# A four-layer conditional network on one core: early blocks in a written-out order, a reordered tail, and 23 products of a constant on TensorE

## The reference, cut to what matters

```python
# x: 16 samples x 128 tokens x 128 features; per sample: two expert numbers, a subject, two angles
h = gelu(x @ Wi[e0] + bi[e0]) @ Wo[e0] + bo[e0] + x         # layer 0, one of 8 experts per sample
x = layernorm(h) * gamma[e0] + beta[e0]
h = layernorm(x) * ln_g + ln_b                              # layer 1
h = (h - mean_over_tokens) / std_over_tokens * gamma(subject) + beta(subject)
gates, idx = top_k(softmax(h @ router_w), 2)                # each token picks 2 of 8 experts
y = sum over the 2 of gate * (relu(h @ w1[e] + b1[e]) @ w2[e] + b2[e])
x = x + y
x = rotate pairs of features by theta and phi               # layer 2
r = gelu(x @ down_W.T + down_b)                             # layer 3, one of 16 experts per sample
x = layernorm((r @ expert_W[e3].T + expert_b[e3] + emb[e3]) @ up_W.T + up_b + x) * gamma3 + beta3
```

## Time and profile before

| | before |
|---|---|
| median of 3 runs (lowest, highest), us | 231.68 (230.59, 233.28) |
| the profiled execution's own time, us | 230.44 |
| its span from the first to the last instruction, us | 228.6 |
| busy: PE, DVE, ACT, POOL, us | 178.3, 116.6, 107.2, 109.0 |
| mean granted TensorE clock, share of full | 0.842 |
| in the chain that ended last: PE, DVE, POOL, issue, DMA | 35%, 21%, 19%, 11%, 9% |

### The profile page before, as it was taken

One profiled execution on the slowest core, in us unless ns is written; L12 is line 12 of the kernel. 1 busy time (PEld: TensorE's weight loads), 2 busy tenths in 40 slices (PEclk: granted clock), 3 DMA queues, 4 the chain that ended last, 5 costly groups with the idle time before them and its releaser, 6 DMA issues.

```text
span 228.6 us, 5312 instructions
## 1 busy us (share of the span) xinstructions
PE 178.3 (78%) x1287; PEld 161.6 (71%) x1287; DVE 116.6 (51%) x575; ACT 107.2 (47%) x338; POOL 109.0 (48%) x126
## 2 busy tenths in 40 slices
PE   6999997999959599284799888887799994077920
PEld 6999986898859599173798777876688873045710
DVE  6316798888943868940023343311236777353460
ACT  3564874665235566301566556564356651123310
POOL 5126335102870670127777777777776333101560
PEclk9999999997667859857589999999999999555555
DMA  6999999994643113047456565535951011330001
GB/s 205 294 322 337 329 317 301 250 292 123 220 130 100 26 34 106 1 104 231 137 154 186 156 173 146 147 97 173 319 167 57 26 46 47 106 134 1 26 25 44
DMA packets 35048, 34.82 MB, mean 152 GB/s; under 512 B 3793, under 2 KB 26475, under 8 KB 35019
## 3 DMA queue, kind: packets, MB, share of 16 engines
q1 hardware_dynamic: 27995, 26.56, 40.3%
q0 software_dynamic: 2496, 5.12, 7.5%
q10 hardware_dynamic: 4528, 2.81, 4.0%
HBM read 29.81 MB, written 4.65 MB: 151 GB/s over the span
## 4 chain that ended last, share of the span: by engine, by line
PE 35%; DVE 21%; POOL 19%; issue 11%; DMA 9%; DVEq 2%; ACT 1%; ACTq 0%; POOLq 0%; SPq 0%
PE bank L808 31%; POOL got L536 7%; POOL token_rows L542 7%; DMA got<-h_rows,src_i 6%; DVE st L1196 3%; PE bank L975 1%; POOL rstd L522 1%; DVE hot_in L1374 1%; POOL rs L556 1%; DVEq L1598 1%; DMA token_rows<-y_blk,dst_i 1%; DMA w_place<-token_rows 1%; DVE y_blk L1475 1%; DVE top_i L1272 1%; PE bank L1004 1%
## 5 line engine op out<-in xcount | busy, mean ns | idle before, releaser
L726 ACT ACTIVATE hid<-bank,small 128x128 f32<-128x128 f32 x156 | 44.4, 368 | 28.0 <-PE bank L808 27.2
L808 PE MATMUL bank<-w,hid 128*128 x312 | 46.5, 297 | 5.3 <-DVE y_blk L1475 4.8
L542 POOL DMA_INDIRECT token_rows<-y_blk,dst_i x39 | 38.8, 995 | 23.0 <-DVE y_blk L1475 13.4
L536 POOL DMA_INDIRECT got<-h_rows,src_i x39 | 38.2, 981 | 22.2 <-issue 10.1
L808 PE MATMUL bank<-gotT,w_now 128*128 128x128 f32 x312 | 46.8, 299 | 0.0
L808 PEld LDWEIGHTS bank<-w,hid 128*128 128x128 f32 x312 | 42.1, 209 | 6.3 <-issue 6.0
L808 PEld LDWEIGHTS bank<-gotT,w_now 128*128 128x128 f32 x312 | 42.9, 213 | 0.0
L1475 DVE TENSOR_TENSOR y_blk<-bank,b_tab 128x128 f32<-128x128 f32 x39 | 11.4, 291 | 58.5 <-PE bank L808 57.0
L975 PE MATMUL bank<-ident,got 128*128 128x128 f32 x39 | 13.0, 334 | 18.0 <-DMA got<-h_rows,src_i 13.2
L716 ACT ACTIVATE gotT<-bank 128x128 f32<-128x128 f32 x39 | 11.0, 282 | 27.2 <-PE bank L975 26.9
L667 ACT ACTIVATE act<-bank,small 128x128 f32<-128x128 f32 x64 | 18.0, 374 | 11.9 <-PE bank L808 11.5
(11 more groups left out here) (232 smaller groups left out, 267.8 us busy)
## 6 DMA issues: line engine op xcount, KB each, us to landing
w_now<-in_exp_w SPq DMA_DIRECT2D x39, 256.0 KB, 3.3
...
```

Source lines behind the costliest of these rows:

```text
L536: g_.indirect_dma_start(got[:, n % RING, :], None, h_dram[0:(HB if n < EARLY else NB) * P], bass.IndirectOffsetOnAxis(ap=src_i[:, n:n + 1] ...
L542: g_.indirect_dma_start(y_dram, bass.IndirectOffsetOnAxis(ap=dst_i[:, n:n + 1], axis=0), y_blk[:, n % YRING, :], None).then_inc(st_y[n % Y ...
L726: last = a_.activation(hid[:, n % HRING, c, :], up_bank(n)[:, c * P:(c + 1) * P], ACT.Relu, bias=cols[:, bass.ds(e * FC + (R_B1 + c), 1)])
L808: return t_.matmul(out_, lhsT, rhs, start=start, stop=stop)
```

## The change

1. Early blocks. What PE, ACT, DVE and POOL do for blocks 0 to 8 and for routing groups 2 and 3 is now written out call by call. DVE no longer adds b2 for these blocks: ACT copies the product (`evac_y`), and POOL adds b2 in `scatter(n)` just before it issues the DMA, with the expert's number loaded into a register first. ACT takes over the normalization of groups 2 and 3 (`norm1`; DVE gives the shift, `minus_mean`). `hot_slots` makes two comparisons of 8 x 128 elements in place of 16 of 128. `experts3(2)` and `experts3(3)`, which prepare layer 3, move behind the early blocks, and the 8 products of `keep_warm` ahead of them are gone. In layer 0 `rows_back` and `store_rows` of groups 0 and 1 come earlier.
2. Tail. BEGIN3 goes from 30 to 34, so units 0 to 3 start four blocks later, and unit 3 ends after the last block. The root of units 1 to 3 and their gain and shift move from DVE to POOL, those of unit 6 from POOL to DVE (`own_norm`). PE loads the experts' numbers of layer 3 ahead of time (`l3_which`). SP stores units 1 to 3 after the last loads.
3. `fill(n)` issues `keep_warm(n)` at six places of the tail: 3 + 12 + 2 + 2 + 2 + 2 = 23 products.

```diff
@@ -50,10 +50,11 @@
-    RING, YRING, TRING, WRING, HRING = 16, 12, 4, 6, 3
+    RING, YRING, TRING, WRING, HRING = 16, 10, 4, 6, 3
...
+    FIRST_OUT = 3
...
@@ -61,7 +62,7 @@
-    BEGIN3 = 30
+    BEGIN3 = 34
...
@@ -468,16 +471,15 @@
-                if n == SETTLED + WRING + 2:
+                if n == SETTLED + WRING + 4:
...
                     for u in range(HU):
                         load_y(u)
-            for u in range(HU):
-                store_out(u)
+            store_out(0)
             scattered(NBLK)
             for u in range(HU, NU):
                 load_y(u)
-            for u in range(HU, NU):
+            for u in range(1, NU):
                 store_out(u)
...
@@ -538,7 +540,14 @@
             def scatter(n):
-                pool.wait_ge(v_y, n + 1)
+                if n < EARLY:
+                    pool.wait_ge(a_y, n + 1)
+                    e = pool.value_load(exp_i[0:1, n:n + 1], min_val=0, max_val=E1 - 1)
+                    ch.do(g_.tensor_tensor(y_blk[:, n, :], y_blk[:, n, :],
+                                           b2_tab[:, bass.ds(e, 1), :].rearrange("p o d -> p (o d)"), ALU.add))
+                    ch.settle()
+                else:
+                    pool.wait_ge(v_y, n - EARLY + 1)
                 g_.indirect_dma_start(y_dram, bass.IndirectOffsetOnAxis(ap=dst_i[:, n:n + 1], axis=0),
                                       y_blk[:, n % YRING, :], None).then_inc(st_y[n % YRING], 16)
...
@@ -578,18 +588,21 @@
-                if n == 2:
+                if n == 3:
                     power(1, 2)
                 if n == 4:
                     power(1, 3)
+                if n == 5:
+                    power(2, 2)
                 if n == 6:
-                    power(2, 2)
-                if n == 7:
                     power(2, 3)
             hot_tiles(1)
-            for n in range(HELD):
+            pool.wait_ge(l_w2, 16 * (E1 + 1))
+            for n in range(FIRST_OUT):
                 scatter(n)
             hot_tiles(2)
+            for n in range(FIRST_OUT, HELD):
+                scatter(n)
             pool.wait_ge(v_idx, 2)
             pool.wait_ge(st_h[2], 16)
             pool.wait_ge(st_h[3], 16)
@@ -599,13 +612,18 @@
                 scatter(n)
                 if n + LEAD < NBLK:
                     gather(n + LEAD)
+            power3(1)
+            power3(2)
+            gain_shift3(1)
+            gain_shift3(2)
+            power3(3)
+            gain_shift3(3)
             power3(HU)
             power3(HU + 1)
             gain_shift3(HU)
             power3(HU + 2)
             gain_shift3(HU + 1)
             power3(HU + 3)
-            gain_shift3(HU + 2)
...
@@ -685,8 +703,8 @@
-                if b == 14:
-                    store_rows(0)
+                if b >= 13 and b < 13 + HG:
+                    store_rows(b - 13)
...
@@ -742,39 +759,61 @@
...
+            def evac_y(n):
+                act.wait_ge(p_y, n + 1)
+                a_.activation(y_blk[:, n, :], y_bank(n), ACT.Copy).then_inc(a_y, 1)
+
             act.wait_ge(v_exp, 1)
-            transposed(0)
-            transposed(1)
-            e = block_expert(0)
-            for k in range(NBLK):
-                if k == EARLY:
-                    transposed(k)
-                    transposed(k + 1)
+            for k in range(EARLY):
+                transposed(k)
+                if k == 2:
+                    norm1(2)
+                if k == 3:
+                    norm1(3)
+                if k == 5:
+                    film_h(2)
+                    film_h(3)
+                hidden(k, block_expert(k))
+                if k >= BEHIND:
+                    evac_y(k - BEHIND)
+                if k == 6:
+                    store_rows(2)
+                if k == 7:
+                    store_rows(3)
+                    hot_rows(1)
+            evac_y(EARLY - 2)
+            evac_y(EARLY - 1)
+            hot_rows(2)
+            evac_m3(2)
+            evac_m3(3)
+            transposed(EARLY)
+            transposed(EARLY + 1)
+            act.wait_ge(v_exp, 2)
+            e = block_expert(EARLY)
+            for k in range(EARLY, NBLK):
...
-                if k == 3:
-                    film_h(2)
-                if k == 4:
-                    film_h(3)
-                    hot_rows(1)
-                if k == 5:
-                    store_rows(2)
-                if k == 6:
-                    store_rows(3)
...
@@ -785,10 +824,15 @@
-                if 2 <= u and odd == 0:
-                    norm3(u - 2)
-            norm3(HU - 1)
+                if k == NBLK - 1:
+                    norm3(0)
+            gelu3(2)
+            evac_uT(3)
+            gelu3(3)
+            norm3(1)
+            norm3(2)
             evac_uT(HU)
+            norm3(3)
             evac_uT(HU + 1)
...
@@ -930,11 +976,11 @@
+                if b == 13:
+                    rows_back(0)
                 if b == 14:
+                    rows_back(1)
                     rank(0)
-                    rows_back(0)
-                if b == 15:
-                    rows_back(1)
...
@@ -962,10 +1010,7 @@
             experts3(0)
             experts3(1)
             inverse(0)
-            experts3(2)
-            experts3(3)
             pe.wait_ge(v_bias, 1)
-            keep_warm(8, bank[6], ident[:])
             pe.wait_ge(l_w2, 16 * (E1 + 1))
...
@@ -1021,9 +1068,15 @@
+            place3 = {}
+
+            def l3_which(u):
+                b, _ = UNITS[u]
+                place3[u] = [pe.value_load(m_idx[0:1, b + k:b + k + 1], min_val=0, max_val=MT - 1) for k in unit(u)]
+
             def l3_up(u):
                 b, n = UNITS[u]
-                which = [pe.value_load(m_idx[0:1, b + k:b + k + 1], min_val=0, max_val=MT - 1) for k in unit(u)]
+                which = place3.pop(u)
...
@@ -1031,52 +1084,72 @@
...
             def down_of(n):
                 e = pe.value_load(exp_i[0:1, n:n + 1], min_val=0, max_val=E1 - 1)
                 blk_down(n, e)
 
-            for k in range(NBLK + BEHIND):
-                if k == EARLY:
-                    down_of(k - 2)
-                    inverse(2)
-                    down_of(k - 1)
-                    pe.wait_ge(v_exp, 2)
-                    rows_T(k)
-                    rows_T(k + 1)
+            pe.wait_ge(v_exp, 1)
+            pe.wait_ge(a_gelu, NB)
+            pe.wait_ge(a_m3, 2)
+            rows_T(0)
...
+            rows_T(3)
+            z_transposes(2)
+            blk_up(3)
+            down_of(1)
+            rows_T(4)
+            z_transposes(3)
+            blk_up(4)
+            down_of(2)
+            rows_T(5)
+            blk_up(5)
+            down_of(3)
+            rows_T(6)
+            route(2)
+            blk_up(6)
+            route(3)
+            down_of(4)
+            rows_T(7)
+            rank(1)
+            rows_back(2)
+            blk_up(7)
+            down_of(5)
+            rows_T(8)
+            rows_back(3)
+            blk_up(8)
+            down_of(6)
+            inverse(1)
+            down_of(7)
+            down_of(8)
+            experts3(2)
+            inverse(2)
+            experts3(3)
+            pe.wait_ge(v_exp, 2)
+            rows_T(EARLY)
+            rows_T(EARLY + 1)
...
@@ -1084,17 +1157,34 @@
+            def fill(n):
+                keep_warm(n, bank[2], ident[:])
+
+            l3_which(HU - 1)
+            l3_down(HU - 1)
+            l3_residual(HU - 1)
+            fill(3)
+            l3_up(HU - 1)
+            l3_which(HU)
+            l3_which(HU + 1)
+            fill(12)
             l3_T(HU)
+            fill(2)
             l3_T(HU + 1)
             l3_down(HU)
             l3_residual(HU)
             l3_T(HU + 2)
+            fill(2)
             l3_up(HU)
+            l3_which(HU + 2)
             l3_down(HU + 1)
             l3_residual(HU + 1)
             l3_T(HU + 3)
+            fill(2)
             l3_up(HU + 1)
+            l3_which(HU + 3)
             l3_down(HU + 2)
+            fill(2)
             l3_residual(HU + 2)
             l3_up(HU + 2)
             l3_down(HU + 3)
...
@@ -1370,10 +1463,11 @@
             def hot_slots(h, first, past):
-                for j in range(first, past):
-                    last = v_.tensor_scalar(hot_in[:, h, j, :], col_bf[:], in_blk[:, j:j + 1], None, ALU.is_equal)
-                    if j % 4 == 3:
-                        last.then_inc(v_hot, 1)
+                n = past - first
+                v_.tensor_tensor(hot_in[:, h, first:past, :],
+                                 col_bf[:].rearrange("p (o n) -> p o n", o=1).to_broadcast([P, n, P]),
+                                 in_blk_bf[:, first:past].rearrange("p (j o) -> p j o", o=1).to_broadcast([P, n, P]),
+                                 ALU.is_equal).then_inc(v_hot, 1)
...
@@ -1588,49 +1682,39 @@
+            minus_mean(2)
             l1_stats(3)
-            l1_norm(2)
-            l1_norm(3)
+            hot_blocks(1)
```

(48 more changed lines are left out.)

154 lines of the change are left out of this document (64 added, 90 removed).

## The result

The changed kernel is slower. Over 20 runs each its median is 234.53 us and that of the kernel before 230.44; the ratio is 1.0192 with a 95% interval of 1.016 to 1.0224, some 4.4 us. (Ratios are formed from undisturbed executions alone, so one can differ a little from that of the medians.) The profiled execution took 233.05 us with a span of 230.9.

The account below looks back on a forecast made before the run. POOL's unbroken issue of late gathers and scatters, then PE, then a serial tail were taken to bound the kernel. 0 + 4.3 - 6.6 - 0.9 = -3.2 us on 231.68 gave 228.5 us, range 226.5 to 230.5 (222.5 to 235.5 with rivals (a), (b)).

Parts of the forecast that it names:

- POOL's stretch: POOL from first to last late gather, 71.2 us before; forecast as a sign to become 75.5 us.
- y: End of DVE's addition of b2 to block 38: 194.80 us before, forecast 188.2 with layer 3 and the root moved.
- End of the early blocks: From the start to the first late gather: gains and losses cancel, 0 us (-3 to +5).
- Additions on POOL: Among the late gathers, five early scatters each gain a register load and an addition: +4.3 us (2.0 to 6.5).
- Move of layer 3 and the root: Last late gather to y: layer 3 behind block 34 and the root off DVE save 6.6 us.
- Tail from y on: From y to the end, fills and PE's clock change the time by -0.9 us (-2.4 to +0.6).
- rival (b): Blocks behind the ranking and fill(12) at half clock: +5 early, tail about +1.5, total 235.9 us; chance 0.2.
- rival (a): PE's clock holds full in the early blocks (-3) and whole tail (-2.4): total 224.0 us; chance 0.22.
- the rule of the Trainium skill: PE's clock gate is closed by default and a busy engine opens it; by it the tail term is -2.4 us.
- the row of 212 to 214: Profile window of the kernel before: PE busy 2.00 of 2.00 us in layer-3 products, yet at 1.2 GHz.
- Its sign: The first late gather coming later than 101.35 + 3.2, about 104.6 us, which decides against the change.
- PE's clock: In the tail, forecast as a sign to be full through fill(12) and to fall later.

Follow-up runs that it names:

- e1: The kernel before with only part 1 of the change (early blocks' order, b2 on POOL, normalization on ACT); ratio to the kernel before 1.0407.
- e4: The changed kernel with unit 0's statistics one block earlier, its root on POOL, and norm3(0) ahead of unit 2's copy; ratio to the kernel before 1.0233.
- e6: The changed kernel without its 23 fill products of the constant; ratio to the kernel before 1.0064.
- e12: The changed kernel run again, unaltered, for a second trace; ratio to the kernel before 1.0247.
- e2: The kernel before with only parts 2 and 3 of the change (later layer 3, roots on POOL, fills); ratio to the kernel before 0.9876.
- e8: The kernel before with 36 products of the constant added ahead of unit 4's first transpose; ratio to the kernel before 1.0008.
- e11: The kernel before's early blocks, with a reworked tail: unit 3 ahead of the last b2 addition, 14 fill products ahead of register loads; ratio 0.9585.
- e13: The changed kernel with 5, 6 and 9 products of the constant ahead of blk_up(6), blk_up(7) and blk_up(8); ratio to the kernel before 1.0044.
- e3: The changed kernel with inverse(1) and inverse(2) ahead of blk_up(8) on PE, and hot_rows(2) right behind hot_rows(1) on ACT; ratio to the kernel before 0.9887.
- e7: e3 with five early scatters, not three, ahead of hot_tiles(2) and six, not four, ahead of the first late gather; ratio to the kernel before 0.972.
- e5: e3 and e4 together, with unit 3's combination and unit 1's normalization taken ahead of the last b2 addition; ratio to the kernel before 0.9567.

## Why the prediction was wrong

The predicted sum was -3.2 us; the stages of the traces add up to about +3.6, for a measured 4.1 to 4.4: the ranking to the first late gather +4.9 (means of 17.56 in the changed order, in the traces of the changed kernel, e1, e4, e6 and e12, and 12.62 in the old one, in those of the kernel before, e2, e8 and e11), less 1.1 by which the ranking itself comes earlier in them (87.0 for 88.0, of which 0.6 is the start up to `z_transposes(0)`), POOL's stretch +2.0 in the same traces, the last gather to y -3.1 (19.55 in the changed kernel, e2, e6 and e12, 22.64 before and in e8), and the tail to the last operation +0.9 (28.24 in the changed kernel and e12, 27.39 before and in e8).

**End of the early blocks, "0 (-3 to +5)": failed, by 3.8 us,** inside its range but near the dear end. The steps behind the ranking were counted rightly, "14 to 15 us of steps in a row", and that is what e13 takes with the clock held. What was wrong was to leave half clock there to a rival with a chance of 0.2. The prediction itself said that ACT would make PE wait in every block, and the earlier trace rows showed that an idle PE loses its clock; together they make the slow case the likely one, and it came in all five traces of this order. Half clock cost 2.4 to 3.1 us there, by e13. Nor did I ask what in this row of steps the source list needs: only the two inverses and `hot_rows(2)`, as e3 showed, 6.4 us earlier.

**Additions on POOL, "+4.3 us (2.0 to 6.5)": mechanism right, size at the lower bound.** The mis-sized term is the register load, at 0.37 us, which I had read on DVE: on POOL nothing of it showed. The addition took 0.46 for 0.49; e7 moved two of the scatters out of the stretch and the end followed, 3.8 us.

**Move of layer 3 and the root, "-6.6 us": failed, by 3.5.** The wrong step is "DVE has one root chain left (unit 0), which it does while PE still has some 5 us to go". PE had these 5 us, but not free of unit 0: its bank was wanted by `l3_residual(2)` ahead of the last product with w2. The root moved, and the wait with it, from DVE's queue to PE's. With the bank freed (e4) and unit 3 ahead (e5) the stage takes 17.4, where the forecast's 188.2 - 172.53 is 15.7. From the transpose of block 38 to the end of the last product with w2 PE took 16.1 us (179.59 to 195.66) where the forecast had 12.5; with the bank freed it takes 14.6 (e4). So the bank is shown for 1.5 of the 3.5 us. Of the rest, e5 still has a hole of 0.61 us ahead of that product, and in six of the seven groups ahead of it (177.13 to 187.26) the four products last 0.99 to 1.11 us, where I had 0.89 for each, some 1.0 us together; why they do no run shows.

**Tail from y on, "-0.9 us": failed, by 1.8.** The first transpose of unit 4 was to be 0.75 us later after y; it was 6.5 later. I took `l3_up(3)` to end 4.7 after y; it ended 8.4 after, as `l3_residual(3)` waits 1.24 us for unit 1 and the products of unit 3 ran at half clock (1.05 to 1.22 us a group for 0.62 to 0.71). `fill(12)` began at half clock too, as rival (b) had it. The clock was then full to the end, as rival (a) had it, and that gave back 5.3; the 3.2 us that I took back there for DVE and the register loads did not come (15.4 us in place of 20.6 - 6.3 + 3.2 = 17.5). So the rule of the Trainium skill that the prediction weighed beside the row of 212 to 214 (TensorE: Matmul & The Clock Gate, Part 1: The HAM clock gate) led right behind that transpose and wrong ahead of it.

Rival (b), 235.9 us at 0.2, was nearest to the measured 234.53: right on both places of half clock. That it came so near is in part luck: it kept the -6.6, 3.5 too much of a gain, and had the early blocks (+5), the additions (+4.3) and the tail (+1.5) too dear by 1.2, 2.3 and 0.6. Its sign, a first late gather behind 104.6, did not come in the first trace (103.64) and came in the second (107.09). Of the other signs, "the first transpose of unit 4 comes more than 9 us after y" came true, and PE's clock came the other way round, half into `fill(12)` and full later; POOL's stretch was 73.1 for 75.5, and b2 of block 38 was added 0.2 us after PE's last product with w2, as said.
